# Cross-attention sums: two PSUM banks in turn, normalised and split in place, turned by DMA, and projected in fp16 pairs

## The chip, the cores and the metric

The kernel runs on one core of one Trainium2 chip. The metric is the device time of one execution in microseconds. Each kernel is written out by hand, one instruction stream per engine: TensorE (PE), ScalarE (ACT), VectorE (DVE), GpSimd (POOL) and SyncE (SP), which issues the DMAs of the steady part.

## The reference, cut to what matters

One decoder layer over 16 batches of 256 tokens, 128 wide: self-attention with one head, cross-attention with 16 heads over a context of 1601 rows of 96, and a feed-forward part that works on 31 chosen tokens of each batch. All but a few per cent of the work is the cross-attention:

```
q = (x @ Wq)          # 16 heads of 64
k = context @ Wk ; v = context @ Wv
attn = softmax(q k^T / 8)
out  = attn @ v       # per head
return out @ Wo + bo
```

The kernel folds the weights: `G` = Wq Wk^T per head, so that queries meet the raw context, and `M` = Wv Wo per head (16 heads x 96 rows = 1536 rows of 128). The attention weights are summed against the context itself, giving 96 numbers per head and token, and these sums are projected by `M`.

## The kernel before

The context of a batch is laid out as 13 tiles of 124 rows. A head pair takes 13 tiles; a batch has 8 head pairs, so 104 tiles, and the 16 batches 1664. For each tile n the streams do the following.

- `st` (L573, L574): TensorE computes the scores of 124 context rows against 512 queries (2 heads x 256 tokens), as two fp16 products, a high and a low part, into PSUM bank 4 or 5.
- ScalarE exponentiates them into the fp32 ring `PF` (L897).
- Every second tile, `round` makes the fp16 high part `EH` of two tiles (L1091 on VectorE for three of four, L904 on ScalarE for the fourth), and `lo` makes the low part `EL` on GpSimd (L1566).
- `av` (L590, L592), eight tiles behind: TensorE adds EH x Ch and EL x Cl into PSUM bank 6, 8 matmuls of 97 columns; the 97th column is the denominator.

Beside these, spread over the tiles, stand the row maxima of the next heads (`diff`, `base`, `fold`: L613, L919, L1114), the queries (`q`: L623, L933, L1123), and "side steps" which all use bank 7 one after another: self-attention of the next batch, the context's transposes, `placemax` (the row maxima, which a small DMA puts into the score operand, L1670), the router's row (`sel_row`, with `sel_count` L1359 to L1361 and `sel_rank` L1368, L1370), the chosen tokens' layer (`c_...`), `turn_u` and `proj`. A side step waits until the one before has been read out of the bank.

What becomes of the sums of a head pair x, before: ScalarE copies bank 6 to `U` (L913), which frees the bank; VectorE takes the reciprocal of the denominators (L1144), two tiles and more after the last `av`; GpSimd multiplies into `Un` (L1574). After two head pairs, `turn_u` (two of them) has TensorE transpose three blocks of 128x128 in fp32 (L646), and ScalarE copies them, scaled, to `UT` (L924). `proj` (L636) multiplies `UT` with `M` in fp32, 6 matmuls into bank 7, and VectorE adds the result to `X` (L1156). The last head pair is normalised straight out of PSUM on VectorE (L1134).

The order of each stream is fixed. `whole_order` puts every step at a tile number, from the tables `SA_PLACES`, `SEL_PLACE`, `TURN_PLACES`, `CHOSEN_PLACES`, and `LATER` shifts a kind of step by some tiles in one engine's stream alone. Each engine executes its own list in order; semaphores join them. `keep_busy` issues idle matmuls (L543) at waits of the start and the end.

## Time and profile before

| | us |
|---|---|
| median of 3 runs | 2164.53 (2164.51 to 2168.09) |
| profiled execution, span from the first to the last instruction | 2169.9 |
| PE busy | 2103.3 |
| POOL busy | 1933.6 |
| ACT busy | 1832.2 |
| DVE busy | 1736.7 |

The page gives the span as the profiled execution's only time. The profile shows one execution. The busy time of an engine is the time in which at least one of its instructions runs; PEld is the load of TensorE's weights, which runs beside its matmuls. An fp32 matmul appears as two instructions, an fp32 transpose as one.

### The profile page before, as it was taken

The numbers are of one execution on the slowest core, as the hardware profiler recorded it, in microseconds if no ns is written. First come the engines' busy times: TensorE is split into PE (matmuls) and PEld (weight loads), VectorE is DVE, ScalarE is ACT, GpSimd is POOL, SyncE is SP. The second block draws the span as 40 slices with busy tenths as digits, with TensorE's granted clock in tenths as the row PEclk, the third lists the DMA queues.
The fourth block names the chain that finished last, engine by engine and source line by source line (L and its number), as shares of the span: only waits on it lengthen the run. The fifth ranks groups of instructions, "written<-read, shape, count | busy, mean of one in ns | idle before, by whom it ended". The sixth has DMA issues, their size and how long they took to land.

```text
span 2169.9 us, 58374 instructions
## 1 busy us (share of the span) xinstructions
PE 2103.3 (97%) x22087; PEld 1544.3 (71%) x22087; DVE 1736.7 (80%) x4158; ACT 1832.2 (84%) x3124; POOL 1933.6 (89%) x1127
## 2 busy tenths in 40 slices
PE   8999999999999999999999999999999999999998
PEld 4677777777777777777777777777777777777665
DVE  7778878787887888879687797878878788886764
ACT  6898898989888888998888888898878888888872
POOL 3899999999999899999899998998989999899991
PEclk9999999999999999999999999999999999999999
DMA  3110000000000000000000000000000000000000
GB/s 73 42 38 13 2 13 2 2 13 2 13 2 2 13 2 13 2 13 2 11 13 2 13 2 2 14 2 13 2 11 13 2 13 2 2 2 2 2 11 11
DMA packets 17366, 22.10 MB, mean 10 GB/s; under 512 B 5872, under 2 KB 14976, under 8 KB 17088
## 3 DMA queue, kind: packets, MB, share of 16 engines
q1 hardware_dynamic: 15984, 18.17, 3.0%
q8 instruction: 177, 2.90, 0.6%
q14 instruction: 101, 0.83, 0.1%
q10 hardware_dynamic: 1104, 0.20, 0.1%
HBM read 16.14 MB, written 2.10 MB: 8 GB/s over the span
## 4 chain that ended last, share of the span: by engine, by line
PE 76%; DVE 11%; issue 5%; ACT 5%; POOL 2%; DMA 0%; SPq 0%; DVEq 0%; ACTq 0%; POOLq 0%
PE PS L573 14%; PE PS L613 13%; PE PS L574 13%; PE PS L590 11%; PE PS L592 10%; PE PS L636 4%; DVE EH L1091 4%; PE PS L646 2%; PE PS L623 2%; DVE over L1114 2%; POOL EL L1566 2%; ACT PF L897 2%; PE PS L657 1%; ACT over L919 1%; DVE junk L1359 1%
## 5 line engine op out<-in xcount | busy, mean ns | idle before, releaser
L1566 POOL TENSOR_TENSOR EL<-PF,EH 124x1024 f16<-124x1024 f32 x828 | 1761.7, 2153 | 144.0 <-DVE EH L1091 69.4
L897 ACT ACTIVATE PF<-PS 124x512 f32<-124x512 f32 x1664 | 972.6, 602 | 203.7 <-PE PS L574 190.1
L590 PE MATMUL PS<-Ch,EH 123*128 123x97 f16 (+1 forms) x6656 | 765.8, 207 | 22.9 <-POOL EL L1566 22.2
L592 PE MATMUL PS<-Cl,EL 123*128 123x97 f16 (+1 forms) x6656 | 762.3, 207 | 0.0
L1091 DVE TENSOR_SCALAR_CACHE_REDUCE EH<-PF 124x1024 f16<-124x1024 f32 x621 | 746.1, 1209 | 18.1 <-ACT PF L897 16.9
L590 PEld LDWEIGHTS PS<-Ch,EH 123*128 123x128 f16 (+1 forms) x6656 | 609.1, 98 | 181.5 <-issue 62.7
L1114 DVE CUSTOM_DVE_ANT_1 over<-over,PS 128x806 f32<-128x806 f32 x512 | 506.6, 989 | 284.7 <-ACT over L919 142.8
L592 PEld LDWEIGHTS PS<-Cl,EL 123*128 123x128 f16 (+1 forms) x6656 | 597.8, 98 | 168.2 <-issue 1.9
L573 PE MATMUL PS<-AH,ChT 97*124 97x512 f16 x1664 | 646.6, 389 | 6.5 <-ACT PF L897 5.8
L574 PE MATMUL PS<-AL,ClT 96*124 96x512 f16 x1664 | 633.7, 381 | 0.0
L919 ACT ACTIVATE over<-PS 128x806 f32<-128x806 f32 x512 | 433.4, 846 | 28.6 <-PE PS L613 8.6
L573 PEld LDWEIGHTS PS<-AH,ChT 97*124 97x124 f16 x1664 | 224.9, 135 | 106.0 <-ACT PF L897 42.5
L613 PE MATMUL PS<-ChT,AH 96*128 96x403 f16 x1024 | 261.8, 337 | 1.3 <-DVE pmax L1114 1.0
L613 PE MATMUL PS<-KD,AH 96*128 96x403 f16 x1024 | 261.6, 336 | 1.5 <-ACT over L919 1.2
L574 PEld LDWEIGHTS PS<-AL,ClT 96*124 96x124 f16 x1664 | 226.6, 136 | 30.4
L904 ACT ACTIVATE EH<-PF 124x1024 f16<-124x1024 f32 x211 | 223.4, 1060 | 0.0
L1123 DVE SCALAR_TENSOR_TENSOR AL<-PS,qscale,AH 96x512 f16<-96x512 f32 x128 | 95.3, 745 | 44.8 <-ACT AH L933 44.8
L1574 POOL TENSOR_TENSOR Un<-U,rden_u 128x384 f32<-128x384 f32 x127 | 112.3, 884 | 18.0 <-DVE rden_u L1144 18.0
L933 ACT ACTIVATE AH<-PS,qscale 96x512 f16<-96x512 f32 x128 | 87.5, 684 | 21.5 <-PE PS L623 20.7
L636 PE MATMUL PS<-M,UT 128*128 128x128 f32 x768 | 100.6, 281 | 0.5
L613 PEld LDWEIGHTS PS<-ChT,AH 96*128 96x128 f16 x1024 | 79.1, 98 | 19.2 <-DVE pmax L1114 4.1
L636 PEld LDWEIGHTS PS<-M,UT 128*128 128x128 f32 x768 | 90.8, 192 | 1.3 <-DVE VX L1424 0.8
(248 smaller groups left out, 1766.9 us busy)
## 6 DMA issues: line engine op xcount, KB each, us to landing
Cf<-in_ctx SPq DMA_DIRECT2D x16, 546.0 KB
X<-in_x SPq DMA_DIRECT2D x16, 128.0 KB, 2.4
out_x<-X SPq DMA_DIRECT2D x16, 128.0 KB, 1.7
msk<-in_attention_mask SPq DMA_DIRECT2D x4, 256.0 KB, 4.3
AH<-mh SPq DMA_DIRECT2D x63, 2.0 KB
Cf<-in_ctx SPq DMA_DIRECT2D x16, 53.6 KB
xWqT<-in_xWqT SPq DMA_DIRECT2D x2, 256.0 KB, 6.5
xWo<-in_xWo SPq DMA_DIRECT2D x2, 256.0 KB, 4.3
```

The source lines that it names most:

```text
L573: pe.matmul(o, ChT[j][:, t, :], AH[:, cs], start=True, stop=False)
L574: pe.matmul(o, ClT[j][:, t, :], AL[:, cs], start=False, stop=True).then_inc(sg("st"), 1)
L590: pe.matmul(PS[:, 6, u0:u0 + DC + 1], EH[0:kr, r, qs], Ch[j][0:kr, t, :], start=(t == 0 and q == 0), stop=False, skip_group_check=True)
L592: m = pe.matmul(PS[:, 6, u0:u0 + DC + 1], EL[0:kr, r, qs], Cl[j][0:kr, t, :], start=False, stop=(t == KT - 1), skip_group_check=True)
L613: m = pe.matmul(PS[:, bank + n, 0:NKEY], AH[0:DC, ht * P:(ht + 1) * P], src[:, n * NKEY:(n + 1) * NKEY], start=True, stop=True)
L636: m = pe.matmul(PS[:, kb, t * D:(t + 1) * D], UT[:, t, c, :], M[:, qd * QC + c, :], start=(c == 0), stop=(c == QC - 1))
L897: act.activation(PF[:, n % PRING, :], PS[0:KP, 4 + n % 2, :], ACT.Exp).then_inc(sg("ex"), 1)
L904: act.activation(EH[:, r - 1:r + 1, :], PF[:, f - 1:f + 1, :], ACT.Copy, scale=KEEP).then_inc(sg("eh_act"), 1)
L919: act.activation(over[:, i % 2, :, :], PS[:, 2:4, 0:NKEY], ACT.Relu).then_inc(sg("relu"), 1)
L1091: dve.tensor_scalar(EH[:, r - 1:r + 1, :], PF[:, f - 1:f + 1, :], KEEP, None, ALU.mult, ALU.add, accum_out=esum[:, r // 2:r // 2 + 1]).the ...
L1114: dve.tensor_tensor_reduce(out=o, in0=o, in1=PS[:, 0:2, 0:NKEY], scale=1.0, scalar=LEAST, op0=ALU.add, op1=ALU.max, accum_out=pmax[:, b % ...
L1566: pool.tensor_tensor(EL[:, r - 1:r + 1, :], PF[:, f - 1:f + 1, :], EH[:, r - 1:r + 1, :], ALU.subtract).then_inc(sg("lo_pool"), 1)
```

## The change

It has five parts that belong together.

1. The sums of head pair x go to bank 6 + x % 2, and the side steps take the other of the two banks while that pair is being summed. A program (`held_before`, `sums_before`, `given_up`) works out whom each user of a bank has to wait for: a side step, or the low part (`ul`) of the pair that had the bank.
2. `norm` moves to the tile where the sums end. VectorE takes the reciprocal and multiplies within PSUM. The copy `U` and GpSimd's product go.
3. `u_split`, one tile later: ScalarE writes the high part of the normalised sums as fp16, VectorE the low part, both into `UHL`.
4. `turn_u`, four tiles after: one DMA issued by SP transposes `UHL` (128 x 1536 fp16) into `UT`. TensorE's transposes and ScalarE's copies go. SP gets an order of its own.
5. `M` is scaled by a power of two and split once, in the first batch (`m_max`, `mtop`, `msplit`), and `proj`, nine tiles after the sums' end (before: five), is 12 fp16 matmuls. VectorE's add to `X` takes back the scale.

Besides, several places and shifts are changed, and `sel_rank` uses other instructions.

```diff
-SA_PLACES = (5, 7, 10, 12, 30, 32, 56)
-SEL_PLACE = 35
-TURN_PLACES = (55, 60, 62, 64)
-SIGMA_PLACE = 72
-CHOSEN_PLACES = (24, 82, 84, 87, 94)
+SA_PLACES = (3, 5, 11, 13, 30, 32, 36, 41, 56)
+SEL_PLACE = 37
+TURN_PLACES = (54, 57, 65, 67)
+SIGMA_PLACE = 71
+M_PLACE = 36
+SPLIT_LATER, TURN_LATER, PROJ_LATER = 1, 4, 9
+CHOSEN_PLACES = (24, 76, 81, 89, 97)
...
+        todo += [(M_PLACE, ("m_max",)), (M_PLACE + 2, ("mtop",)), (M_PLACE + 5, ("msplit",))]
...
-        if done >= 2 and (done - 2) % KT == 0:
-            put(n, "norm", (done - 2) // KT)
-        for late, step in ((-2, ("turn_u", 0)), (2, ("turn_u", 1)), (5, ("proj",))):
...
+        if done >= 0 and done % KT == 0 and done // KT < B * HP - 1:
+            put(n, "norm", done // KT)
+        if done >= 0 and done % KT == SPLIT_LATER:
+            put(n, "u_split", done // KT)
+        for later, kind in ((TURN_LATER, "turn_u"), (PROJ_LATER, "proj")):
+            if done >= 0 and done % (2 * KT) == KT + later:
...
-                ("turn_u", B - 1, QD - 1, 0): 4, ("proj", B - 1, QD - 1): 1, ("sel_row", B - 1): 17,
+                ("proj", B - 1, QD - 1): 24, ("sel_row", B - 1): 17,
...
# TensorE
-                        w.wait_ge(sg("u"), b * HP + hp)
+                        w.wait_ge(*given_up(sums_before[x]))
...
                         for c in range(QC):
-                            m = pe.matmul(PS[:, kb, t * D:(t + 1) * D], UT[:, t, c, :], M[:, qd * QC + c, :],
-                                          start=(c == 0), stop=(c == QC - 1))
+                            for part, of in enumerate((MH, ML)):
+                                m = pe.matmul(PS[:, kb, t * D:(t + 1) * D], UT[:, (part * T + t) * QC + c, :],
+                                              of[:, qd * QC + c, :], start=(c == 0 and part == 0),
+                                              stop=(c == QC - 1 and part == 1))
...
# ScalarE
-                        act.activation(U[x % 2][:, :, :], PS[:, 6, 0:4 * (DC + 1)].rearrange(
-                            "p (q c) -> p q c", c=DC + 1), ACT.Copy).then_inc(sg("u"), 1)
...
-                    act.activation(UT[:, t, :, :], PS[:, bank_of(s), 0:QC * P].rearrange("p (c q) -> p c q", q=P),
-                                   ACT.Copy, scale=u_scale[:, b % 4:b % 4 + 1]).then_inc(sg("ut"), 1)
+                elif k == "u_split":
...
+                    w.wait_ge(sg("un"), x + 1)
+                    w.wait_ge(sg("ut"), 16 * max(0, b * QD + qd - 1))
+                    act.activation(
+                        UHL[qd % 2][:, 0, :, 2 * (x % 2):2 * (x % 2) + 2, :].rearrange("p t h c -> p h t c"),
+                        sums_bank(x)[:, :, 0:DC].rearrange("p (h t) c -> p h t c", t=T),
+                        ACT.Copy, scale=KEEP).then_inc(sg("uh"), 1)
+                elif k == "msplit":
+                    w.wait_ge(sg("m_scale"), 1)
+                    act.activation(M[:, :, :], M[:, :, :], ACT.Copy, scale=mscale[:, 0:1]).then_inc(sg("m_scaled"), 1)
+                    w.wait_ge(sg("m_scaled"), 1)
+                    act.activation(MH[:, :, :], M[:, :, :], ACT.Copy, scale=REST).then_inc(sg("m_hi"), 1)
...
# VectorE
+                    w.wait_ge(sg("av"), (x + 1) * KT)
+                    dve.reciprocal(rden_u[:, x % 2, :], sums[:, :, DC]).then_inc(sg("u_r"), 1)
+                    w.wait_ge(sg("u_r"), x + 1)
+                    dve.tensor_tensor(sums[:, :, 0:DC], sums[:, :, 0:DC],
+                                      rden_u[:, x % 2, :].rearrange("p (q o) -> p q o", o=1).to_broadcast([P, 4, DC]),
+                                      ALU.mult).then_inc(sg("un"), 1)
+                elif k == "u_split":
...
+                    dve.tensor_tensor(UHL[qd % 2][:, 1, :, hs, :].rearrange("p t h c -> p h t c"),
+                                      sums_bank(x)[:, :, 0:DC].rearrange("p (h t) c -> p h t c", t=T),
+                                      UHL[qd % 2][:, 0, :, hs, :].rearrange("p t h c -> p h t c"),
+                                      ALU.subtract).then_inc(sg("ul"), 1)
...
+                    dve.scalar_tensor_tensor(out=X[:, T * b:T * b + T, :],
+                                             in0=PS[:, bank_of(s), 0:T * D].rearrange("p (t d) -> p t d", d=D),
+                                             scalar=back, in1=X[:, T * b:T * b + T, :],
+                                             op0=ALU.mult, op1=ALU.add).then_inc(sg("pj_x"), 1)
...
-                    dve.tensor_tensor_reduce(out=rank[:, j, :], in0=cnt[:, j, 0, :], in1=cnt[:, j, 2, :], scale=1.0,
-                                             scalar=0.0, op0=ALU.add, op1=ALU.add, accum_out=spill())
-                    dve.tensor_scalar(keep[:, j, :], cnt[:, j, 1, :], NSEL + 0.5, None,
-                                      ALU.is_gt).then_inc(*own_step())
+                    for t in range(T):
+                        dve.tensor_scalar(rank[:, j, t:t + 1], cnt[:, j, 0, t:t + 1], cnt[:, j, 2, t:t + 1], None,
+                                          ALU.add, ALU.add, accum_out=spill())
+                    dve.tensor_scalar(keep[:, j, :], cnt[:, j, 1, :], NSEL + 0.5, None, ALU.is_gt, ALU.add,
+                                      accum_out=spill()).then_inc(*own_step())
...
# SyncE
-            for s in order:
+            for s in orders["sp"]:
...
+                elif k == "turn_u":
+                    b, qd = s.a
+                    w.wait_ge(sg("ul"), b * HP + 2 * qd + 2)
+                    w.wait_ge(sg("pj_mm"), b * QD + qd)
+                    sp.dma_start(UT[:, :, :], UHL[qd % 2][:, :, :, :, :].rearrange("p w t h c -> p (w t h c)"),
+                                 transpose=True).then_inc(sg("ut"), 16)
```

## Rows read from the trace of the kernel before

**Rows 1.** The page: span and busy time of each engine.
```profile
span 2169.9 us, 58374 instructions
PE 2103.3 (97%) x22087; PEld 1544.3 (71%) x22087; DVE 1736.7 (80%) x4158; ACT 1832.2 (84%) x3124; POOL 1933.6 (89%) x1127
```

**Rows 2.** TensorE's waits: what waited, for what: us in total, times, longest.
```profile
PE PS L590 <- POOL EL L1566: 22.2, 36, 1.1
PE PS L573 <- ACT PF L897: 5.8, 14, 1.4
```

**Rows 3.** The page: the chain that ended last, by engine.
```profile
PE 76%; DVE 11%; issue 5%; ACT 5%; POOL 2%; DMA 0%; SPq 0%; DVEq 0%; ACTq 0%; POOLq 0%
```

**Rows 4.** Groups by shape, TensorE: count | busy us, mean ns | idle before, releaser.
```profile
L636 PE MATMUL PS<-M,UT 128*128 128x128 f32 x768 | 100.6, 281 | 0.5
L646 PE MATMUL PS<-ident,Un 128*128 128x128 f32 x384 | 65.5, 280 | 0.9 <-ACT mh L948 0.9
...
L646 PEld LDWEIGHTS PS<-ident,Un 128*128 128x128 f32 x384 | 44.1, 143 | 11.6 <-issue 6.9
```

**Rows 5.** TensorE in order of time: start us, us, instruction.
```profile
1006.30 0.51 PE L646 MATMUL PS<-ident,Un 128*128 128x128 f32 x3
1006.65 0.38 PE L573 MATMUL PS<-AH,ChT 97*124 97x512 f16 x1
...
1009.40 0.20 PE L592 MATMUL PS<-Cl,EL 123*128 123x97 f16 x1
...
1009.66 0.21 PE L592 MATMUL PS<-Cl,EL 123*128 123x97 f16 x1
1009.70 1.57 PE L636 MATMUL PS<-M,UT 128*128 128x128 f32 x12
1011.11 0.38 PE L573 MATMUL PS<-AH,ChT 97*124 97x512 f16 x1
```

**Rows 6.** Busy us by stretch: length, PE, PEld, DVE, ACT, POOL, PEclk, DMA share, GB/s.
```profile
995.00:1000.00 5.00, 3.73 (x38) 2.41 (x37) 5.00 (x14) 2.84 (x5) 5.00 (x4) 1.00 0.00 0
...
1065.00:1070.00 5.00, 3.33 (x21) 2.28 (x22) 2.68 (x8) 2.41 (x5) 3.74 (x2) 0.81 0.08 27
```

**Rows 7.** Groups by shape, VectorE.
```profile
L1114 DVE CUSTOM_DVE_ANT_1 over<-over,PS 128x806 f32<-128x806 f32 x512 | 506.6, 989 | 284.7 <-ACT over L919 142.8 <-PE PS L613 139.2 <-issue 0.3
...
L1370 DVE TENSOR_SCALAR keep<-cnt 128x2 f32<-128x2 f32 x16 | 32.7, 2042 | 0.0
...
L1193 DVE SCALAR_TENSOR_TENSOR Cl<-Ch,Cf 124x672 f16<-124x672 f16 x16 | 23.8, 1488 | 0.0
...
L1144 DVE RECIPROCAL rden_u<-U 128x4 f32<-128x4 f32 x127 | 21.8, 172 | 3.1 <-ACT U L913 3.1
...
L1368 DVE CUSTOM_DVE_ANT_0 rank<-cnt 128x2 f32<-128x2 f32 x16 | 10.7, 668 | 0.0
...
L1349 DVE TENSOR_SCALAR_CACHE_REDUCE X<-wraw,rbc 128x2 f32<-128x2 f32 x16 | 3.3, 209 | 0.0
...
L1299 DVE SCALAR_TENSOR_TENSOR G<-PS,gscale,G 128x384 f16<-128x384 f32 x4 | 2.3, 610 | 0.0
```

**Rows 8.** Groups by shape, ScalarE and GpSimd.
```profile
L924 ACT ACTIVATE UT<-PS,u_scale 128x384 f32<-128x384 f32 x127 | 74.9, 590 | 15.2 <-PE PS L646 12.0
L913 ACT ACTIVATE U<-PS 128x388 f32<-128x388 f32 x127 | 62.3, 490 | 0.0
L953 ACT ACTIVATE Cf<-Cf,sigma 124x1248 f32<-124x1248 f32 x15 | 20.4, 1357 | 0.0
...
L1574 POOL TENSOR_TENSOR Un<-U,rden_u 128x384 f32<-128x384 f32 x127 | 112.3, 884 | 18.0 <-DVE rden_u L1144 18.0
```

**Rows 9.** In order of time, the last head pair's sums and projection.
```profile
2127.92 0.56 DVE L1134 TENSOR_TENSOR Un<-PS,rden_u 128x384 f32<-128x384 f32 x1
...
2129.77 1.60 PE L636 MATMUL PS<-M,UT 128*128 128x128 f32 x12
```

**Rows 10.** DMA issues: count, KB each, median us from issue to landing.
```profile
msk<-in_attention_mask SPq DMA_DIRECT2D x4, 256.0 KB, 4.3
...
xWqT<-in_xWqT SPq DMA_DIRECT2D x2, 256.0 KB, 6.5
```

216 lines of the change are left out of this document (107 added, 109 removed).

## Prediction

> **What bounds the kernel now.** I read the page's busy times first, then TensorE's waits, the chain that ended last, the groups by shape, a few stretches instruction by instruction, and the DMA issues. TensorE is busy for 2103.3 of 2169.9 us, 66.6 us short of the span; GpSimd follows with 1933.6, ScalarE with 1832.2 and VectorE with 1736.7 [rows 1]. TensorE's longest recorded wait is 22.2 us in all, for `EL` from GpSimd, and its waits for the scores' exponentials come to 5.8 us [rows 2]. The chain that ended last is TensorE for 76% of its length, VectorE for 11% [rows 3]. "Busy" could hide slack, since matmul ends are modelled, so I looked at starts: within a step of the weighted sums the starts run from 1009.40 to 1009.66 in six equal steps, 0.043 us for 97 columns, and the next step's matmul follows without a gap [rows 5]. So TensorE sets the pace through the 15 batches of the steady part, and time taken from it is worth nearly its full length until the next engine is late. That engine is VectorE in one stretch of each batch: from 995 to 1000 us of the span VectorE is busy for all 5 us, GpSimd too, and TensorE only for 3.73 [rows 6]. There the router counts delay `EH`, this delays `EL`, and this the weighted sums.
>
> **What it removes from TensorE.** (a) The projection's six fp32 matmuls show as twelve instructions, 64 times, 768 in all [rows 4]. One group starts at 1009.70 and the next scores at 1011.11, a slot of 1.41 us [rows 5]. Twelve fp16 matmuls of 128 columns take its place. The trace has this shape only next to it: 97 columns in 0.043 us, so 128/97 x 0.0433 = 0.057 us each, 0.69 us for twelve. Bounds: nothing saved, if the two-part products ran as slowly as the two-part fp32 ones, and 1.41 - 12 x 0.043 = 0.89 us saved if a matmul costs the same at 128 columns. I take 1.41 - 0.69 = 0.72 us x 64 = 46 us, being close to the row of the same type. (b) The 384 transposes of `Un` go [rows 4]; three of them occupy 1006.30 to 1006.65, 0.35 us [rows 5], x 128 = 45 us. (c) The weight-load queue stood idle 6.9 us on "issue" before these transposes [rows 4], which goes too. Together 46 + 45 + 7 = 98 us, 4.5% of the span.
>
> **What it removes and adds elsewhere.**
> ScalarE loses the copy of the sums (62.3 us) and the copy of the turned sums (74.9 us) [rows 8] and gains 128 high parts of 384 columns. The nearest rows give 0.49 (388 columns, fp32 out) and 0.58 us (384, fp32 out, with a scale from a tile) [rows 8]; at 0.55 us that is 70 us, so ScalarE goes to about 1832 - 137 + 70 = 1765.
> GpSimd loses the normalising product, 112.3 us [rows 8], and its 18 us wait: 1821 us.
> VectorE gains 128 products in PSUM. The last head pair does this product already, out of PSUM, in 0.56 us [rows 9]: 72 us. It gains 128 subtractions for the low parts, between 0.56 [rows 9] and 0.61 us [rows 7]: 73 us, and 16 small scales at 0.21 plus an accumulator read, 5 us. It loses the rank and keep instructions of the choice: 0.67 + 2.04 us per batch, whose replacements are three of the kind that takes 0.21 us, plus reads, about 0.9: 1.9 x 16 = 31 us less [rows 7]. Sum 1737 + 72 + 73 + 5 - 31 + 6 (preparing `M`) = 1862 us, 89% of the new span against 80%.
> No new engine passes TensorE's 2103 - 91 = 2012 us. But three things couple more tightly.
> (d) The normalisation now stands at the very position where the sums end, and ScalarE's high part one position later waits for it. Behind that ScalarE instruction wait the exponentials, and TensorE runs two scores ahead of these at most. The sums end, VectorE takes 0.17 + 0.56 us [rows 7, 9] plus hand-over, and up to another 1.2 us (one `EH`) if it is behind; ScalarE reaches its instruction about one tile (1.3 us) after. So ScalarE stalls between 0 and 0.9 us per pair, and the two score banks give TensorE about as much cover as one exponential is ahead. Bounds: 0, and 0.9 x 128 = 115 us if the cover were gone. Since TensorE waited only 5.8 us for exponentials in all [rows 2], I take the low end's side: 8 us.
> (e) In the stretch where VectorE limits, its extra 1.13 us per pair shows in full: up to 1.1 x 16 = 18 us. The 1.9 us taken off the choice comes after that stretch and helps only partly; the bound on the other side is a gain of 1.27 x 16 = 20 us, if that stretch's gap closed because GpSimd is now free of the 0.88 us product. I take +8.
> (f) A side step now takes the bank that the pair before has just left and waits for that pair's low part. The self-attention values, the router row and three of the five places of the chosen tokens lie two positions behind the change of bank, so some 40 steps can wait; VectorE must be within 2.6 us of TensorE. Bounds 0 and 40 us (1 us each); I take 4.
> (g) `M` is scaled and split once, at position 41 of the first batch, and the first projection stands at 42. Scaling 1536 columns on ScalarE twice is 2 x 1.36 x 1536/1248 = 3.3 us [rows 8], the low part on VectorE 1.49 x 1536/672 = 3.4 us [rows 7]. TensorE stands behind it for most of this: 5 us, bounds 0 and 8.
> (h) At the end the last product ends at 2128.48 and the projection starts at 2129.77 [rows 9]. Instead come a high part, a low part (1.1 us) and the DMA; with a DMA of 4.5 us the projection starts at about 2134.2 and is 0.7 us shorter: +4 us, bounds +2 and +9.
> (i) The queue on SP now holds the transposing DMA, which waits for the low part, ahead of the row maxima. These are due nine positions (11 us) later, so I cost this at nothing; without that cover each of the 64 rows could hold the scores up.
>
> **The DMA.** One transfer turns 128 partitions x 1536 fp16 values, 393 KB, per two head pairs. TensorE wants it nine positions after the second pair's sums end: 9 x 1.25 = 11.2 us in the shorter period. The low part is ready 2.2 us after the sums at best and, with a queue of one instruction on each engine in front, some 4 us after; so 7 to 9 us are left. The trace has no transposing DMA. Plain ones of 256 KB took 4.3 and 6.5 us from issue to landing [rows 10]; as both contain a fixed part, 393 KB should take between 4.3 and 6.5 x 393/256 = 10.0 us. I take 5.5, which is covered; the upper end is not.
> The Trainium skill has two rules that disagree here. "VectorE: DVE Perf Modes", The three transpose paths, gives 1309 ns for a 128x128 turn by DMA; were the twelve blocks of this transfer done one after another at that, it would be an estimated 15.7 us, some 7.5 us late at each of 64 projections, and the time about 2570 us. "Advanced Engine Details and Errata", X-Bar Transpose, says that transposing transfers are as fast as ordinary ones, with 350 to 400 GB/s: an estimated 1.1 us beside the fixed part, and nothing late. No row here can tell which; the first is the same rival as B below, at a higher price.
>
> **Sum.** Idle 66.6 - 6.9 + 8 + 8 + 4 + 5 + 4 = 88.7 us, busy 2103.3 - 91 = 2012.3: a span of 2101.0, 68.9 us less than the profiled execution's 2169.9. That span is 5.4 us above the 2164.5 us median of the unprofiled runs. Taking the difference from that, 2164.5 - 69 = 2095.5; I forecast **2095 us**. Its own range is 2066 (everything removed, nothing given back: 2164.5 - 98) to 2120 (the terms d to h at twice their sum and a little more).
>
> **Rivals.**
> A: VectorE becomes the bound. For it: 89% load, the fully used stretch of rows 6, and new instructions that sit on the way to the exponentials. Against it: 285 us of its idle time lie before the row-maximum fold [rows 7], where it only waits for work that comes earlier if TensorE is faster. If a third to a half of its 145 us of new work shows on the path, the gain is 98 - 48 - 9 (g, h) = 41 us down to 98 - 72 - 9 = 17 us: 2124 to 2148.
> B: the transfer lands late, which ends slower than before. At 10 us behind a low part at 4 us it lands at 14 against 11.2: TensorE stands 2.8 us at 64 projections, 179 us, giving 2095 + 179 = 2274. It decides at 69/64 = 1.1 us of delay per projection, so at a transfer of about 8.3 us. For it: rows of 6.5 us for less data. Against: those were issued close together at the start, several sharing the engines, where now the engines are nearly idle. Standing still also costs clock: after such a gap TensorE's granted clock is 0.81 in a stretch of 5 us in which it worked for 3.33, between its two levels (1.2 and 2.4 GHz) [rows 6].
> C: the fp16 pairs save nothing over the fp32 halves (the change doesn't do what it says). Then only 45 + 7 us go and 29 come back: 2141. Against it stands the 0.043 us row.
>
> **Chances.** Forecast 0.66, A 0.18, B 0.10, C 0.03, and 0.03 for something that brings it under 2066. From no change within 0.2% (4.3 us, about what can be told here) I count 0.02, taken from the ends of A and B. Faster 0.86, same 0.02, slower 0.12 (B and the worst of A). The range is 2062 to 2150: it holds the forecast, most of A and C.
>
> **What would show it.** Right: no PE rows for `Un`, twelve fp16 projection matmuls starting 0.057 us apart, TensorE busy near 2012 us, the DMA landing in under 7 us with no wait of TensorE for it save the last; GpSimd near 1821, VectorE near 1860. Waits of ScalarE for the normalisation under 1 us each, mostly covered. Wrong: TensorE waiting for DMA before each projection (B); rows of the projection still 0.117 us apart (C); TensorE idle over 120 us, on `EL`, exponentials or the low part, with VectorE over 95% busy between (A).

## The result, and the profile after

| | before | after |
|---|---|---|
| median, us (lowest to highest of 4 runs) | 2165.5 (2164.5 to 2168.1) | 2467.1 (2462.2 to 2469.7) |
| profiled execution, span | 2169.9 | 2460.9 |
| PE busy | 2103.3 | 2147.8 |
| PE, span less busy | 66.6 | 313.1 |
| mean granted clock of TensorE, share of full | 0.997 | 0.953 |

The changed kernel takes 1.1383 [1.1366, 1.1400] times as long: 13.8% slower where 3% faster was forecast, and outside the range. The busy times of VectorE and GpSimd came out near what was worked out, ScalarE's 39 us above it; the page's second line answers to [rows 1] like this:

```profile
span 2460.9 us, 57394 instructions
PE 2147.8 (87%) x21723; PEld 1525.8 (62%) x21723; DVE 1862.1 (76%) x4499; ACT 1803.9 (73%) x3000; POOL 1835.8 (75%) x1000
```

Every engine is now idle for 13% or more of the span, and none is the bound. The loss stands in TensorE's waits (line, what it waited for, us in all, times, longest), to be read against [rows 2]:

```profile
PE PS L598 <- ACT PF L915: 67.4, 115, 1.7
PE PS L671 <- DVE AL L1140: 65.0, 30, 3.8
PE PS L671 <- DVE X2T L1295: 37.9, 14, 3.1
PE PS L649 <- ACT ex L994: 31.4, 14, 2.2
PE PS L678 <- DVE X L1196: 19.2, 15, 1.4
```

The first is the scores waiting until ScalarE has taken the exponentials out of their PSUM bank (5.8 us before). The other four are side steps waiting for another side step to be read out of the bank, on VectorE above all. The waits of ScalarE and VectorE show what the hand-over of the sums does. ScalarE stands 75.5 us for the normalised sums, up to 3.4 us at a time, and exponentials are queued behind it:

```profile
ACT UHL L934 <- DVE PS L1149: 75.5, 62, 3.4
DVE UHL L1157 <- ACT UHL L934: 41.0, 65, 1.6
```

The groups by shape (count | busy us, mean ns | idle before, releaser) carry the durations that the sum was made of:

```profile
L660 PE MATMUL PS<-MH,UT 128*128 128x128 f16 x384 | 51.2, 222 | 17.9 <-DVE AL L1140 9.3 <-DVE X L1284 3.9 <-ACT ClT L957 2.7
L1149 DVE TENSOR_TENSOR PS<-PS,rden_u 128x384 f32<-128x384 f32 x128 | 72.5, 566 | 4.4
L1157 DVE TENSOR_TENSOR UHL<-PS,UHL 128x384 f16<-128x384 f32 x128 | 70.6, 551 | 41.0 <-ACT UHL L934 41.0
L934 ACT ACTIVATE UHL<-PS 128x384 f16<-128x384 f32 x128 | 63.2, 494 | 75.6 <-DVE PS L1149 75.5
L1424 DVE SCALAR_TENSOR_TENSOR X<-X,keep 128x128 f32<-128x128 f32 x32 | 44.6, 1428 | 0.0
...
UT<-UHL SPq DMA_TRANSPOSE x64, 3.7
```

The last line is the page's DMA row: the turning transfer lands 3.7 us after its issue.

**One hand-over.** In order of time (start us, us, instruction, [idle before, releaser]), from the last matmul of a pair's sums to the low part's turn:

```profile
1125.18 0.21 PE L618 MATMUL PS<-Cl,EL 123*128 123x97 f16 x1
...
1126.89 1.21 DVE L1108 TENSOR_SCALAR_CACHE_REDUCE EH<-PF 124x1024 f16<-124x1024 f32 x1
...
1128.03 0.99 DVE L1131 CUSTOM_DVE_ANT_1 over<-over,PS 128x806 f32<-128x806 f32 x1
...
1128.94 0.17 DVE L1147 RECIPROCAL rden_u<-PS 128x4 f32<-128x4 f32 x1
...
1129.15 0.57 DVE L1149 TENSOR_TENSOR PS<-PS,rden_u 128x384 f32<-128x384 f32 x1
...
1129.75 0.49 ACT L934 ACTIVATE UHL<-PS 128x384 f16<-128x384 f32 x1 [2.95 <-DVE PS L1149]
1130.14 0.25 DVE L1254 BATCH_NORM_AGGREGATE mv<-stats 128x2 f32<-128x6 f32 x2
1130.14 0.59 ACT L915 ACTIVATE PF<-PS 124x512 f32<-124x512 f32 x1
```

The sums' last matmul ends at 1125.39 and the reciprocal starts at 1128.94, 3.55 us later: VectorE does the rest of one `EH`, the self-attention's output, another `EH` and a row maximum first. ScalarE has stood 2.95 us, and the next exponential starts only behind the high part. Counted over all 128 pairs, the reciprocal starts 1.47 us after the last matmul's end in the median, more than 1.2 us for 76 of them and more than 2.2 us for 16.

**One side step.** VectorE is at the chosen tokens' input (L1424) while GpSimd's `EL` runs; then `EH`, the row maximum and the queries' low part `AL` have to come in their order, and a context transpose (L671) that has been put one tile behind the query step waits for all of it:

```profile
1151.36 4.27 POOL L1609 TENSOR_TENSOR EL<-PF,EH 124x1024 f16<-124x1024 f32 x2
...
1153.58 2.21 DVE L1424 SCALAR_TENSOR_TENSOR X<-X,keep 128x128 f32<-128x128 f32 x1
...
1155.72 1.21 DVE L1108 TENSOR_SCALAR_CACHE_REDUCE EH<-PF 124x1024 f16<-124x1024 f32 x1
...
1156.86 0.98 DVE L1131 CUSTOM_DVE_ANT_1 over<-over,PS 128x806 f32<-128x806 f32 x1
...
1157.77 0.74 DVE L1140 SCALAR_TENSOR_TENSOR AL<-PS,qscale,AH 96x512 f16<-96x512 f32 x1
...
1158.66 0.55 PE L671 MATMUL PS<-identb,Ch 124*96 124x124 f16 x7 [3.63 <-DVE AL L1140]
...
1167.23 0.83 PE L671 MATMUL PS<-identb,Ch 124*96 124x124 f16 x6 [3.11 <-DVE X2T L1295]
```

The windows over this place (us, then busy us of PE, PEld, DVE, ACT, POOL, granted clock, DMA share, GB/s) show what such a stall leaves behind:

```profile
1150.00:1155.00 5.00, 5.00 (x59) 3.71 (x56) 4.96 (x18) 4.76 (x9) 4.89 (x3) 1.00 0.00 0
1155.00:1160.00 5.00, 1.37 (x15) 1.07 (x15) 4.64 (x9) 1.25 (x3) 2.98 (x3) 0.94 0.00 0
1160.00:1165.00 5.00, 4.12 (x32) 2.77 (x29) 1.75 (x3) 3.04 (x6) 2.58 (x2) 0.72 0.01 3
1165.00:1170.00 5.00, 2.77 (x18) 2.07 (x19) 2.66 (x5) 1.38 (x2) 2.12 (x1) 0.62 0.00 0
```

TensorE works for 1.37 of 5 us; in the next two windows, the second with another stall of 3.11 us, the granted clock is 0.72 and 0.62 in the mean, between its levels of 1.2 and 2.4 GHz, and a score matmul there takes 0.63 instead of 0.38 us.

To see where the loss lies I compared the starts of the scores, tile by tile, over batches 1 to 13: a batch is 19.4 us longer, the balance of 34.4 us of longer tiles and 14.9 us of shorter ones (above all 25, 51, 77 and 103, where the projection used to be, with 1.2 to 1.5 us each). The largest losses are 4.45 us at tile 54, 3.70 at 57, 2.34 at 14, 1.53 at 43, 1.12 at 16, 1.35 and 1.00 at 67 and 68, 1.38 each at 36 and 37, and 1.14 and 1.11 at 8 and 76. Most are places of side steps: transposes at 54, 57, 67; projection at 16 and 42, placed directly ahead of `placemax` at 17 and 43.

**A correction to the text ahead of the prediction.** It says that the projection stood "five" tiles after the sums' end before. In both traces' order it stood 18 tiles after (tiles 25, 51, 77, 103 of a batch, each two tiles ahead of a query step), and stands 9 after in the changed kernel (16, 42, 68, 94). So the change moves the projection forward by nine tiles, in between the query steps at 14, 40, 66, 92 and `placemax` at 17, 43, 69, 95. Four more steps of a batch stand where the bank was crowded already, and the prediction never weighed it.

### The profile page after: what moved, and what is told of

It is laid out like the page before. It is cut to its first block and busy times, and to the rows that moved or that the text cites. A ratio compares the mean times of both kernels' runs of the same rounds, so it can differ in the third digit from the quotient of the medians.

```text
span 2460.9 us, 57394 instructions
## 1 busy us (share of the span) xinstructions
PE 2147.8 (87%) x21723; PEld 1525.8 (62%) x21723; DVE 1862.1 (76%) x4499; ACT 1803.9 (73%) x3000; POOL 1835.8 (75%) x1000
## 5 line engine op out<-in xcount | busy, mean ns | idle before, releaser
L1609 POOL TENSOR_TENSOR EL<-PF,EH 124x1024 f16<-124x1024 f32 x828 | 1766.4, 2150 | 536.3 <-DVE EH L1108 253.0
L616 PE MATMUL PS<-Ch,EH 123*128 123x97 f16 (+1 forms) x6656 | 789.6, 211 | 17.2 <-POOL EL L1609 7.4
L618 PE MATMUL PS<-Cl,EL 123*128 123x97 f16 (+1 forms) x6656 | 785.7, 210 | 0.0
L598 PE MATMUL PS<-AH,ChT 97*124 97x512 f16 x1664 | 671.9, 404 | 77.8 <-ACT PF L915 67.4
L618 PEld LDWEIGHTS PS<-Cl,EL 123*128 123x128 f16 (+1 forms) x6656 | 615.4, 100 | 190.7 <-issue 24.0
L616 PEld LDWEIGHTS PS<-Ch,EH 123*128 123x128 f16 (+1 forms) x6656 | 627.1, 100 | 171.5 <-issue 44.8
L599 PE MATMUL PS<-AL,ClT 96*124 96x512 f16 x1664 | 655.9, 394 | 0.0
L598 PEld LDWEIGHTS PS<-AH,ChT 97*124 97x124 f16 x1664 | 233.9, 141 | 212.4 <-ACT PF L915 142.6
L649 PE MATMUL PS<-X2T,G 128*96 128x256 f16 x512 | 79.7, 278 | 47.6 <-ACT ex L994 31.4
L934 ACT ACTIVATE UHL<-PS 128x384 f16<-128x384 f32 x128 | 63.2, 494 | 75.6 <-DVE PS L1149 75.5
L671 PE MATMUL PS<-identb,Ch 124*96 124x124 f16 x208 | 23.8, 277 | 90.0 <-DVE AL L1140 52.1
L957 ACT ACTIVATE ChT<-PS 96x868 f16<-96x868 f16 (+1 forms) x32 | 26.7, 837 | 102.6 <-PE PS L671 102.5
```

The costliest lines, as they stand in the source:

```text
L598: pe.matmul(o, ChT[j][:, t, :], AH[:, cs], start=True, stop=False)
L599: pe.matmul(o, ClT[j][:, t, :], AL[:, cs], start=False, stop=True).then_inc(sg("st"), 1)
L616: pe.matmul(PS[:, 6 + x % 2, u0:u0 + DC + 1], EH[0:kr, r, qs], Ch[j][0:kr, t, :], start=(t == 0 and q == 0), stop=False, skip_group_check= ...
L618: m = pe.matmul(PS[:, 6 + x % 2, u0:u0 + DC + 1], EL[0:kr, r, qs], Cl[j][0:kr, t, :], start=False, stop=(t == KT - 1), skip_group_check=True)
L1609: pool.tensor_tensor(EL[:, r - 1:r + 1, :], PF[:, f - 1:f + 1, :], EH[:, r - 1:r + 1, :], ALU.subtract).then_inc(sg("lo_pool"), 1)
```

## Experiments

Ratios are to the kernel before, run in turn on the same chip. Theories: **places** (what costs is where the side steps stand), **hand-over** (the chain sums, VectorE, ScalarE, VectorE that now holds the bank), **load** (VectorE's 125 us of new work, the prediction's rival A), and **premise** (whether time off TensorE is worth its length at all).

### What time off TensorE is worth, and what load on VectorE costs

`e9_fp16_only` is the kernel before with `M` and `UT` in fp16 and 12 fp16 matmuls. It leaves out the low parts of both.

```diff
-        M = sb("M", [P, MC, D])
+        M = sb("M", [P, MC, D], F16)
-        UT = sb("UT", [P, T, QC, P])
+        UT = sb("UT", [P, T, QC, P], F16)
+                            for part in range(2):
+                                m = pe.matmul(... UT[:, t, c, :], M[:, qd * QC + c, :], ...)
```

> The kernel before with M and the turned sums kept in fp16 and the projection as twelve fp16 matmuls; the low parts are left out (each product is done twice with the high parts), so no other engine has more work. It measures the projection's term and the premise by themselves. My term: 0.72 us x 64 = 46 us less, about 2165 - 46 + 3 = 2122 us. If TensorE does not set the pace over its full length (rival: the pace is set in turn by VectorE, GpSimd and ScalarE, and time taken from TensorE is worth a part), 2140 us or more.

2152.1 us, 0.9927 [0.9907, 0.9946]. PE busy fell by 40.6 us, the time by 0.73% or 16 us (12 to 20). Its waits took the rest (5.8 to 11.5 for `PF`, 22.2 to 26.1 for `EL`, and 10.2 new for `X`):

```profile
PE 2062.7 (96%) x22087; PEld 1498.2 (70%) x22087; DVE 1747.7 (81%) x4158; ACT 1829.4 (85%) x3124; POOL 1930.8 (90%) x1127
```
```profile
PE PS L590 <- POOL EL L1567: 26.1, 45, 1.1
PE PS L573 <- ACT PF L898: 11.5, 28, 1.4
PE PS L623 <- DVE X L1157: 10.2, 15, 0.7
```

By position: 0.73 us are gained at tile 51, the projection's, and 0.73 us given back at tile 53, the next query step, which waits for VectorE to have read the projection. About four tenths of what is taken off TensorE arrives here (3 to 5 tenths by the interval).

`e5_pairs` does part 5 of the change alone and whole in the kernel before, split of `M` and of the turned sums included (the low part of `UT` by VectorE, out of PSUM).

```diff
+                            for part, of in enumerate((MH, ML)):
+                                m = pe.matmul(PS[...], UT[...], of[:, qd * QC + c, :], ...)
```

> The kernel before with one part of the change alone: the projection in fp16 pairs. TensorE still transposes; ScalarE writes the high part of the turned sums, VectorE the low part; M is split once. Bank 7 alone serves the side steps, bank 6 the sums, all places are those of before. Theory of places: what TensorE is spared comes through, 0.72 us x 64 = 46 us less 5 to 15 us that 72 us more work on VectorE and the longer hold of the bank give back: about 2165 - 35 = 2130 us. Rival, VectorE is the bound whatever the places (rival A of the prediction): 72 us more on it cost half of that, 2165 - 46 + 36 + 20 = 2175 us or more.

2177.6 us, 1.0033 [1.0023, 1.0043]: no gain, in the rival's field, where by the prediction 46 us of TensorE's work had gone. PE busy is 30.9 us less, VectorE has 60.9 us more, and the new waits are 12.8 us for `UT` and 12.2 us for `X`, both on VectorE.

`e18_load` is the kernel before with two idle VectorE instructions behind each pair's reciprocal. No other engine waits for their results, but what stands behind them in VectorE's queue does.

```diff
                     dve.reciprocal(rden_u[:, x % 2, :], U[x % 2][:, :, DC]).then_inc(sg("u_r"), 1)
+                    for _ in range(2):
+                        dve.tensor_scalar(idle_out[:, :], idle_in[:, :], 1.0, None, ALU.mult, ALU.add, ...)
```

> The kernel before with nothing changed but load on VectorE: behind each of the 127 reciprocals two more instructions on 128x384 fp32 whose results nobody reads (some 0.5 us each, about 140 us in all, what the change gave VectorE in products). No new wait between engines and no other place. Theory (what hurts is where a new product stands in a chain of hand-overs, and that the side steps crowd; load by itself is mostly absorbed by VectorE's idle time before the row-maximum fold): 2168 to 2185, VectorE busy near 1865. Rival (rival A of the prediction: VectorE's load binds, a third to a half of it on the path): 2210 to 2235. TensorE's waits for AL, X and X2T would grow under the rival.

2212.5 us, 1.0198 [1.0183, 1.0213]: the rival's number, and my theory's is out. The page:

```profile
PE 2120.5 (96%) x22087; PEld 1551.0 (70%) x22087; DVE 1857.3 (84%) x4667; ACT 1835.0 (83%) x3124; POOL 1935.7 (87%) x1127
```

120.6 us more on VectorE at 84% load cost 44 us, 36% of them, spread over waits of 10 to 15 us (`junk`, `X`, `pmax`). So load is not absorbed, though VectorE is idle 16% of the time. With `e9` this gives an estimated exchange in this kernel: a microsecond off TensorE brings about 0.4, a microsecond onto VectorE costs 0.36. Each rate comes from one run with the work at one place, and no run shows how far it holds elsewhere; `e5` agrees with both (30.9 us off and 60.9 on come to 10 us lost, 9 measured against the kernel before in turn). The change took 91 us off one and put 125 on the other: by these rates about 36 gained and 45 lost, before any hand-over or place is counted, so no gain was left to begin with.

### The mechanism at the places of before

`e16_banks_before` keeps before's banks, the copy to `U`, GpSimd's product and all places, and adds only: high part on ScalarE, low part on VectorE out of `U`, the turning DMA, fp16 pairs.

```diff
+                    act.activation(UHL[...hi...], U[x % 2][...], ACT.Copy, scale=KEEP).then_inc(sg("uh"), 1)
+                    dve.tensor_tensor(UHL[...lo...], U[x % 2][...], UHL[...hi...], ALU.subtract)
-                    m = pe.transpose(...)                     # turn_u on TensorE, and ScalarE's copy
+                    sp.dma_start(UT[:, :, :], UHL[qd % 2][...], transpose=True)
```

> The kernel before with its own banks (6 for the sums, 7 for the side steps), its own way of the sums (ScalarE's copy, reciprocal, GpSimd's product) and its own timetable, and the rest of the change: high part by ScalarE and low part by VectorE out of SBUF, the turn by DMA, the projection in fp16 pairs 18 tiles after the sums. TensorE does the same work as in the changed kernel. If the banks in turn and the chain on them are the cause of what e13 and e14 still lost, this is at or below the kernel before; with the pass-through of e9 (17 of 46 us) the 98 us taken from TensorE give up to 36, less VectorE's 71 to 190 us of new products with two SBUF inputs: 2140 to 2170 us. If the parts, the DMA or the pairs are to blame, 2220 or more.

2223.1 us, 1.0258 [1.0244, 1.0272]: in the upper field, so the banks are not all that `e13` and `e14` still lose. VectorE has 164 us more, of which one group is most:

```profile
L1156 DVE TENSOR_TENSOR UHL<-U,UHL 128x384 f16<-128x384 f32 x128 | 154.8, 1209 | 46.8 <-ACT UHL L924 45.7
```

and by the 0.36 of `e18` 164 us cost 59, against some 36 gained on TensorE. That leaves 35 of the 58 us to other causes; TensorE's largest waits are 39.0 us for `EL` and 23.5 us for `X`, and GpSimd is 32 us busier than before.

`e17_low_on_pool` is the same with that low part on GpSimd.

```diff
-                    dve.tensor_tensor(UHL[...lo...], U[x % 2][...], UHL[...hi...], ALU.subtract)
+                    pool.tensor_tensor(UHL[...lo...], U[x % 2][...], UHL[...hi...], ALU.subtract)
```

> As e16 with the low part on GpSimd, so that VectorE does nothing more than before; GpSimd goes to about 1933 + 128 x 0.83 = 2040 us busy. If VectorE is what binds beside TensorE, 2135 to 2150 us and faster than e16. If GpSimd binds, its wait for EL, 22 us in the kernel before, grows past 60 and it ends at 2180 or more.

2268.2 us, 1.0462 [1.0439, 1.0484]. Against `e16` VectorE has 80 us less (still 84 more than in the kernel before) and GpSimd 68 us more, at 2033.6, and it is 45 us slower; TensorE waits for GpSimd:

```profile
PE PS L597 <- POOL EL L1598: 89.3, 152, 1.6
```

`e13_old_times` is the changed kernel, banks in turn and sums normalised in PSUM, with before's places and shifts and the projection 18 tiles after (only the router's row stays at 37).

```diff
-SA_PLACES = (3, 5, 11, 13, 30, 32, 36, 41, 56)
+SA_PLACES = (5, 7, 10, 12, 30, 32, 36, 41, 56)
-TURN_PLACES = (54, 57, 65, 67)
+TURN_PLACES = (55, 60, 62, 64)
-SPLIT_LATER, TURN_LATER, PROJ_LATER = 1, 4, 9
-CHOSEN_PLACES = (24, 76, 81, 89, 97)
+SPLIT_LATER, TURN_LATER, PROJ_LATER = 1, 4, 18
+CHOSEN_PLACES = (24, 82, 84, 87, 94)
```

> The changed mechanism untouched (two banks, sums normalised and split in PSUM, DMA, fp16 pairs) with the timetable of before: self-attention, transposes, sigma and the chosen tokens at their old places and shifts, the projection 18 tiles behind the sums as before. Only the router's row stays at 37, since at 35 it would wait in a circle. Theory that the timetable is all of the loss: at or below 2165 us, and down to 2140, since e9 showed that 46 us off TensorE bring 17. Theory that the mechanism has a loss of its own (banks in turn, ScalarE held by the normalisation, 60 us of waits for exponentials in e7): 2200 to 2230 us.

2304.4 us, 1.0633 [1.0614, 1.0653], well above both fields. More than half of the loss is gone with the places alone; TensorE still waits 50.3 us for `PF` and now 41.7 us for `X`. `e14_old_times_release` adds to it that VectorE normalises into SBUF, which gives the bank up at once, with ScalarE's high part two tiles and the low part, now on GpSimd, four tiles later, and the router's row and the choice of tokens two tiles earlier, at before's 35 and 48.

```diff
-            return (sg("ul"), holder[1] + 1) if holder[0] == "sums" else left(holder)
+            return (sg("un"), holder[1] + 1) if holder[0] == "sums" else left(holder)
-                    dve.tensor_tensor(sums[:, :, 0:DC], sums[:, :, 0:DC], ...)
+                    dve.tensor_tensor(Un[x % 2][:, :, :], sums[:, :, 0:DC], ...)
```

> As e13 with the normalised sums written to SBUF and the bank given up there, ScalarE's high part two tiles later, GpSimd's low part, and the router's row at 35 too: the side steps of the kernel before at exactly its places. If ScalarE's wait for the normalisation is what is left in e13, this is 30 us faster than e13, about 2150; if only the banks in turn cost (the next pair's sums wait for a side step in their bank), it is within 10 us of e13.

2235.9 us, 1.0316 [1.0298, 1.0334]. The two rows that answer to the hand-over:

```profile
PE PS L599 <- ACT PF L916: 10.3, 34, 1.1
```
```profile
ACT UHL L935 <- DVE Un L1152: 14.5, 20, 3.9
```

So this package is worth 68 us at before's places, more than the 30 expected, though the time is 86 us above the 2150 forecast. What in it does the work is not separated. The reciprocal does not come earlier (1.47 us behind the sums in the median, 1.41 in `e13`); what frees ScalarE is that its high part stands behind the tenth exponential after the pair's own, where it stood behind the ninth in the changed kernel and in `e13`. Whether that shift alone would do, with the bank still held, was not run. What is left is within 13 us of before's banks (`e16`, which differs in who does the low part too). `e15_clear_switch` moves one more transpose off the change of bank, from 60 to 59.

> As e14 with the second group of transposes at 59 instead of 60, so that ScalarE has read it before the next pair's sums want its bank at 61 (in e7 TensorE waited 18 us there, 15 times). If that wait is what the two banks cost, 15 to 25 us less than e14: about 2130 us, faster than the kernel before. If the step then waits for the residual's turn at 56, no change.

2230.4 us, 1.0295 [1.0275, 1.0314], 100 us above the forecast and no more than the runs' spread below `e14`; TensorE's wait for `ChT` went from 19.2 to 11.9 us and little else moved.

### The places by themselves

`e10_before_turn` changes one line of the kernel before.

```diff
-TURN_PLACES = (55, 60, 62, 64)
+TURN_PLACES = (54, 57, 65, 67)
```

> The kernel before with nothing but the context's transposes at the changed kernel's places (54, 57, 65, 67 instead of 55, 60, 62, 64). Theory of places: a transpose step one tile behind a query step (53) and one behind the transposed residual (56) waits for VectorE in any kernel; undoing this in the changed kernel gave 117 us, so the kernel before should lose much of that, 2240 to 2290 us. Rival (the places hurt only with two banks in turn and a VectorE that is behind with the sums): under 2190 us.

2239.0 us, 1.0323 [1.0306, 1.0341], at the low end of what was expected: 70 us for four numbers in a table, with no instruction added. Both waits are on VectorE, which is 7 us less busy than before:

```profile
PE PS L657 <- DVE AL L1123: 30.2, 30, 1.2
PE PS L657 <- DVE X2T L1253: 24.6, 14, 1.8
```

`e1_turn` is the reverse line in the changed kernel.

> The changed kernel with the context's transposes back at their places of before (55, 60, 62, 64 instead of 54, 57, 65, 67), nothing else. Theory of places (the stalls come from side steps that stand one tile behind another that VectorE has yet to read out of the bank): the 103 us of TensorE's waits before L671 go, and with them a like share of the slow clock (busy time rose by 136 us over my 2012 for 246 us more idle time, so 0.55 us per us of wait): 2467 - 103 x 1.5 = about 2310 us. Rival, hand-over of the banks (the two banks in turn are what makes side steps wait, wherever they stand): the waits only move to the next side step, over 2430 us.

2350.5 us, 1.0837 [1.0813, 1.0860]: 117 us back, 40 less than expected. The losses at 54 and 57 (8.2 us a batch) went, and 2.6 us at 55 came: the first transpose at 55 still waits for `AL`, 34.9 us in all. `e3_proj11` puts the projection two tiles on (`PROJ_LATER = 11`), behind `placemax` instead of ahead of it.

> The changed kernel with the projection eleven instead of nine tiles after the sums' end, so that it stands behind the row maxima and not between a query step and them. Theory of places: TensorE's waits of 19.2 us before the row maxima (for the projection's add) and 12 us before the projection (for the query's low part) go; about 2467 - 31 x 1.5 = 2420 us. Rival, the transfer lands too late: then the two tiles more would take away its waits too and the gain is larger; the trace shows 2.4 us of such waits, so this should add nothing.

2424.6 us, 1.1183 [1.1163, 1.1203], as expected. `e7_places` has both, and the self-attention at 10 and 12 again.

> The changed kernel with three places moved: the context's transposes as before, the projection eleven tiles after the sums' end, and the self-attention's values and scores at 10 and 12 instead of 11 and 13, so that the softmax's bank is read before the query step wants it (TensorE waited 31.4 us there, <- ACT ex). If the gains add up (-117 and -43 us measured, 31 x 1.5 = 47 us more): 2467 - 117 - 43 - 47 = 2260 us. If removing one wait only lengthens the next, 2320 us.

2296.3 us, 1.0578 [1.0562, 1.0594], between the 2260 of gains that add up and the rival's 2320: if `e1` and `e3` add up (160 us), the self-attention's places bring 11 us of the 47 hoped for. In `e11_rank_later` the choice of tokens (`sel_rank`, with L1424) also goes from tile 50 to 74, away from the transposes.

> The kernel of e7 with one more place moved: the choice's rank and keep (VectorE, with two products that waited for GpSimd up to 2.2 us each) at tile 74 instead of 50. By position, e7 loses 2.8 us per batch at tile 55, where the transposes wait for VectorE's low part of the query of tile 53. Theory that VectorE's backlog of that moment does it (sums at 46 to 48, rank at 50, query at 54): most of 2.8 us x 15 = 42 us goes, 2296 - 35 = 2260 us. If instead the chain query, ScalarE, VectorE is simply longer than two tiles, no change.

2258.3 us, 1.0404 [1.0380, 1.0429], as expected: the wait for `AL`, 38.9 us in `e7`, is gone, with no instruction less.

### The hand-over in the changed kernel, and the clock

`e2_split` was to move high and low part one tile later.

```diff
-            ... "sa_qk": 2, "sa_t": -1, "sa_turn": 1},                      # ScalarE
+            ... "sa_qk": 2, "sa_t": -1, "sa_turn": 1, "u_split": 1},
-            ... "sigma": -1, "u_split": 1},                                 # VectorE
+            ... "sigma": -1, "u_split": 2},
```

> The changed kernel with the high and the low part one tile later in ScalarE's and VectorE's order, nothing else. Theory that ScalarE, held by the normalisation, holds up the exponentials: ScalarE's 75.5 us of waits for it shrink below 25 and TensorE's 67 us for exponentials below 20; with the clock's share 2467 - 50 x 1.5 = about 2390 us. Rival: the bank is given up a tile later and the side steps behind the change of bank wait longer, so no gain or a loss, 2460 to 2500 us.

2497.0 us, 1.1520 [1.1500, 1.1539]: slower still, but the run does not test its theory. In both traces ScalarE executes its 3000 instructions in the same order, the high part behind the ninth exponential: a step with `LATER` 1 comes first in the next tile, and here nothing of ScalarE's lay between. So its wait for the normalised sums stayed at 74.7 us and TensorE's for `PF` at 66.7. Only VectorE's low part moved, in 47 more of the 128 pairs to behind an `EH`, and the 30 us come with that: the query step's wait on the bank (L649) rose from 31.4 to 49.5 us. `e6_release` is the changed kernel with the early release of `e14`, but with smaller shifts: 1 and 2 for ScalarE's high and GpSimd's low part instead of 2 and 4, the DMA at 5 instead of 7.

> The changed kernel, all places as they are, but the normalised sums are written to SBUF, the bank is given up there, ScalarE's high part comes one tile later out of SBUF, and GpSimd makes the low part (VectorE is spared 71 us). Theory that the chain VectorE, ScalarE, VectorE on the sums in PSUM costs (my point d, 67 us of TensorE's waits for exponentials, with the clock's share 100 us): ScalarE's 75 us of waits for the normalisation fall below 20, time 2370 to 2400. Theory of places alone: the side steps still wait for VectorE as they stand, 2430 or more.

2480.6 us, 1.1430 [1.1413, 1.1447]: no gain, in the upper field. TensorE stands for `AL` and `X2T` as before (68.3 and 40.0 us), and GpSimd has 109 us more. Again ScalarE's order is that of the changed kernel, and its wait for the sums is 78.0 us, where `e14` has 14.5. So giving up the bank early, with the low part on GpSimd, gains nothing here by itself, and what it brings together with a later high part at the changed places was not run. `e8_both` has the shifts of `e14` (2, 4 and 7), the early release, and the places of `e7` but for the self-attention's.

> The early give-up of the bank out of SBUF together with the transposes' places of before and the projection at eleven tiles; the self-attention's places stay as changed. If places and the chain on the sums are two causes that add up: 2467 - 160 - 80 = 2230 us; if VectorE's backlog is the one cause behind both, one of them takes the other's gain and it stays at 2290 or above. Under 2165 us would need the whole idle time gone and is not expected.

2308.3 us, 1.0635 [1.0619, 1.0651], above the 2290 from which VectorE's backlog was to be the one cause behind both. ScalarE's wait for the sums is down to 11.5 us and TensorE's for `PF` halves (60.4 in `e7` to 31.3 us), but the one for `AL` grows (38.9 to 46.9), and the time is 12 us above `e7`'s. `e12_spread` has `e8`'s release, the transposes at 59, 62, 64 and 73 and the choice at 74.

> All that the places by position suggest, together with the early give-up of the bank out of SBUF (ScalarE's high part at three tiles, GpSimd's low part at five): transposes at 59, 62, 64, 73, rank at 74, projection at eleven, self-attention's values and scores at 10 and 12. If the loss is the sum of such local waits, those of e7 at 36 to 38 (3.3 us a batch), 55 (2.8) and 61 (1.3) go: 2296 - 7 x 15 = about 2190 us, still short of the kernel before. If VectorE's load decides, 2260 or more.

2234.4 us, 1.0303 [1.0278, 1.0328], 44 us above what I hoped for and under the rival's 2260. No version that does all the work beats the kernel before.

`e4_fill` fills the waits ahead of two transpose groups of the changed kernel with 10 idle matmuls each.

```diff
+        for bb in range(1, B):
+            STREAM_BUSY |= {("ctx_t", bb, 0, 0, 7): 10, ("ctx_t", bb, 0, 7, KT): 10}
```

> The changed kernel with ten idle matmuls (0.213 us each) ahead of two of the four groups of context transposes of each batch, into the free score bank, so that most of TensorE's wait there is worked through. All waits stay. Theory that half of the loss is TensorE's clock, which falls after it has stood still: the fast clock holds there and the time falls by up to 136 x 103/246 = 57 us, to about 2410. Rival (the lower clock has no part, or is only a by-product of a busy-time reckoning): 2467 or more, since 30 x 2 x 0.213 x 10 = 128 us of work is added, part of it outside the waits.

2408.2 us, 1.1115 [1.1094, 1.1136]: 59 us less by giving TensorE 300 more matmuls, as expected, with the mean granted clock at 0.982 instead of 0.953. So a fifth of the loss goes when these waits are filled. Most likely it is the clock's answer to them, which the windows above show at one place; of the 1664 high-part score matmuls (L598), those over 0.45 us went from 105 to 39.

## Why the prediction was wrong

**Its premise.** "TensorE sets the pace, and time taken from it is worth nearly its full length" fails. The first witness is the busy share. Rows of 0.20 us that start 0.043 us apart [rows 5] mean that each stall is entered with a row still counted as busy. I took for every pair of neighbouring matmul kinds (line and shape) the spacing of starts that a fifth of them undercut, and summed over all 22087: by this estimate TensorE of the kernel before needs 2027 us of the span's 2169.9, which leaves 143 us of slack and not 66.6 (113 us with the median spacing). The Trainium skill says the same from the other side ("TensorE: Matmul & The Clock Gate": a matmul's drain overlaps its successor's fill, so that the gap between starts is shorter than one matmul's latency); the trace agrees with 0.043 against 0.20. The second witness is `e9`: four tenths arrive. The trace of before already spoke for it, with four engines at 80% or more and 285 us of VectorE's idle time ended by one partner or the other [rows 7]: such a loop of engines has no single bound. And the weight of 0.12 that the forecast gave to a slower kernel lay almost all with B, the late transfer, which did not come.

**(a) and (b), TensorE's saving: the sizes were right; (c) was misread.** From start to next start the projection's matmuls took 90.1 us and take 44.3, a saving of 45.8 (46 said); they start 0.056 us apart in the median (0.057 said). The transposes' 45.8 us are gone (45 said). Rival C is out. The 6.9 us of (c) are idle time of the weight-load queue; the matmul engine stood only 0.9 us before these transposes [rows 4], so they were no part of its 66.6 us. And busy PE is 2147.8, not 2012: rows lengthen with stalls and at the lower clock. `e16`, where TensorE executes as many instructions with a mean clock of 0.997, has 2060.1.

**The loads were about right, their price was not.** The products took 0.566 and 0.551 us (0.56 and 0.56 to 0.61 said), ScalarE's high part 0.494 us (0.55 said), and GpSimd is busy for 1835.8 us (1821 said). That VectorE's 1862 came out as 1862.1 is luck: around the choice of tokens 12 us more were spent instead of 31 less (below), which shorter instructions elsewhere (15 us for `KD`, 10 us for `Cl`) and more overlap of neighbouring ones made good. ScalarE's 1803.9 us are 39 above the 1765 said; its instructions' durations summed did fall by 76 us, but fewer of them overlap the next, so its busy time fell by only 28. (e) priced 125 us on VectorE at 8 us, since it looked at one stretch; by the rate of `e18` it is about 45. Rival A had the right rule, a third to a half of it, and too much to set against it: it was given 98 us of TensorE's saving in full.

**(d), the hand-over, is the mis-sized term of the mechanism.** 8 us were said, with 115 as the bound. TensorE waits 67.4 us for `PF`, ScalarE 75.5 us for the sums, and `e13` to `e14` prices early release, a later high part, the low part on GpSimd and the router's row together at 68 us. The argument that before had only 5.8 us of such waits was no evidence: then ScalarE's largest wait for VectorE in the steady part was 7.4 us in all (for `nm`). The text let VectorE be at most one `EH` (1.2 us) behind; the reciprocal started 1.47 us after the sums in the median and up to 4.0 us, and one `EH` and one row maximum in the queue are already 2.2 us.

**(f), the side steps, is the step that failed most.** It asked only whether a side step waits for the pair's low part (4 us, bound 40) and costed the moved places at nothing. Each side step waits for the one before, and that is read out mostly by VectorE. Four places in a table cost 70 us in the kernel before (`e10`) and 117 in the changed one (`e1`); the projection at 9 instead of 18 tiles costs 42 by two tiles of it (`e3`). Of the 302 us lost, 163 go with the places (after to `e13`) and 68 with the package of `e14`. The last 70 are, by argument and not by a run of their own, what is left of load and premise: `e16` has 58 without any new bank.

**The choice of tokens.** The 31 us were saved where they were said to be, and lost again beside it. The keep instruction's mean of 2.04 us [rows 7] was mostly a wait: it now takes 0.15 us, and the instruction of the same step that reads two SBUF tensors, L1424, went from 0.35 us to 1.43 in the mean (348 to 2207 ns, 34.5 us in all), another of that kind, L1384, from 0.29 to 0.57 (9.0 us). The new instructions alone do not explain the move: in `e5`, whose keep instruction is before's, it takes 0.16 us too and the other 1.01. One such wait, 2.21 us beside the running `EL`, stands in the middle of the crowded stretch above; `e11` shows 38 us for putting the step elsewhere, though the instruction still takes 1.33 us there.

**The DMA and the ends: right.** The tail of the changed kernel, in order of time, answers to [rows 9]:

```profile
2411.32 0.57 DVE L1149 TENSOR_TENSOR PS<-PS,rden_u 128x384 f32<-128x384 f32 x1
2411.92 0.49 ACT L934 ACTIVATE UHL<-PS 128x384 f16<-128x384 f32 x1 [3.38 <-DVE PS L1149]
2412.44 0.56 DVE L1157 TENSOR_TENSOR UHL<-PS,UHL 128x384 f16<-128x384 f32 x1 [0.56 <-ACT UHL L934]
2413.03 1.55 SPq L1700 DMA_TRANSPOSE UT<-UHL  x1
...
2417.23 0.23 PE L660 MATMUL PS<-MH,UT 128*128 128x128 f16 x1 [0.98 <-DMA UT<-UHL]
2417.30 0.22 PE L660 MATMUL PS<-ML,UT 128*128 128x128 f16 x1
```

From the product's end to the projection it is 5.3 us (5.7 said, 1.3 before); it is the only one of 64 transfers for which TensorE has a recorded wait. Rival B is out, and with it the dearer of the Trainium skill's two rules: "VectorE: DVE Perf Modes", The three transpose paths, would have made 15.7 us of these 12 blocks, and 3.7 were measured. That leaves room for the other rule, "Advanced Engine Details and Errata", X-Bar Transpose, with its estimated 1.1 us beside a fixed part, which no run here separates. (g) is about right too: in `e16` the first batch is 8.9 us longer than before and the mean later one 2.6, so some 6 us (5 said). (i) was rightly nothing: no wait of TensorE for the row maxima's DMA appears in its list. Three figures of the text do not agree among themselves, which changes nothing in this account: the terms (d) to (h) at twice their sum give 2124 us, not 2120; the 15.7 us transfer would be 8.5 us late and give 2640 us with the low part at 4 us, as B has it, not 7.5 and 2570; and (h) takes the DMA at 4.5 us where the section on it takes 5.5.

**What stays open.** How the last 70 us divide was not taken apart further than `e5`, `e16`, `e17` and `e18` do; of the 58 of `e16`, 35 lie beyond both exchange rates. Which part of the package of `e14` brings its 68 us is open. Whether a timetable worked out afresh for the new mechanism would reach 2165 us is open too; those tried did not.

## What to carry to other kernels

When four engines each stand at 80% or more and hand work round in a ring, price an edit by an exchange rate measured in that kernel (take 40 us off one engine, put 120 on another) before adding microseconds; here both rates were near four tenths, at the places where they were measured. Take "busy" of a pipelined engine from the spacing of starts, not from the share. And read moved places in a table as the change's first part: for each step moved, name who must read out the step ahead of it, what is in that engine's queue at that tile, and count in tiles from the trace rather than from the code's offsets. The trace of an experiment also tells whether its edit moved what it was to move: two shifts by one tile left ScalarE's order as it was.

## What the runs showed of the hardware

- The same VectorE product (128x384, a subtraction to fp16) takes 0.55 us with one input in PSUM (L1157: 525 to 559 ns) and 1.21 us in the mean with both in SBUF (`e16`, L1156: 542 to 2568 ns). Of the 128, 125 start while GpSimd's `EL` runs, and all but one of these end 0.41 to 0.43 us after that instruction does (correlation of its length with GpSimd's remaining time 0.94). The Trainium skill has the rule: "SBUF — State Buffer", SBUF: two separate sides, calls the port pair of VectorE and GpSimd an exclusive lock, held for a whole instruction, for VectorE operations with two SBUF inputs. The trace agrees, and it means that a long GpSimd instruction nearly always running added 0.66 us in the mean to each such operation here. L1424 and L1384 read two SBUF tensors and fit it; the keep instruction reads only one, and no run here shows what it waited for.
- After 3.6 us without work TensorE's granted clock was 0.72 and 0.62 in the following windows of 5 us, the latter with a further stall of 3.1 us; filling two such waits per batch by 10 matmuls each gave 59 us back.
- A DMA that turns 128 x 1536 fp16 values lands in 3.7 us (median of 64), 4.2 us at the end between issue and first use.
